# Third power of the far distance on GpSimd, parts of the near sum and of an edge mask on VectorE, in a convolution and spline kernel

## The chip, the cores and the metric

The kernel runs on one core of one Trainium2 chip. The metric is the device time of one execution in microseconds (us). Engines are named as in the profile: PE is TensorE, PEld its weight load, DVE is VectorE, ACT is ScalarE, POOL is GpSimd, SP is SyncE, which here only issues transfers.

## The reference

The input x has shape (32, 64, 56, 56). First comes a residual block with two 3x3 convolutions whose weights are replaced by their signs, each with a batch norm over the whole batch. Then each pixel goes through a cubic spline whose table of 32 knots is mixed per channel.

```python
out = relu(batchnorm(conv3x3(x, sign(w1)), gamma1, beta1))
x = relu(batchnorm(conv3x3(out, sign(w2)), gamma2, beta2) + x)
...
x_aff = clip(x * a + b, -1.5, 1.5)
u = (x_aff + 1) * 0.5 * (K - 1)              # K = 32
i = floor(u); t = clip(u - i, 0, 1)
spline = sum over k in 0..3 of alpha_table[clip(i - 1 + k, 0, 31)] * b_k(t)   # cubic B-spline basis
y_nl = einsum('bchwr,cr->bchw', spline, mix)
return id_gain * x + y_nl + bias
```

## The kernel before

Partitions hold 64 channels of two images. The function `convolutions` does both convolutions pair by pair, keeps the results in scratch tensors in HBM and builds the spline's coefficients beside them. The function `spline` then does the rest in 32 chunks (CHUNKS) of 1568 pixels (CHUNK, half an image), and almost all of the change is there.

Near a knot the spline is a cubic in the signed distance from that knot. For each pixel five coefficients are needed; the code calls them tables and numbers them T_NEAR, T_FAR, T_SQ, T_LIN and T_VAL: third power near the knot, third power of the distance beyond one cell (the far part), square, slope, value. A table is summed on PE: masks say which steps a pixel has passed, and matmuls of the masks with diagonal matrices of coefficient steps add the steps up in PSUM. There are four masks for each chunk. Two "middle" masks are made by VectorE (`middle`) and two "edge" masks by ScalarE (`edge`); each has four blocks of 1568 pixels. T_NEAR and T_FAR use all four masks and need 128 matmuls each, the others use the two edge masks and need 64 each, 448 together. Two PSUM tiles `tab` take turns, so PE may start a table when VectorE has consumed the one two before it (semaphore `table_used`).

VectorE consumes a table by adding the base and multiplying by a power of the distance, reading PSUM and one tile of SBUF: `near_cube`, `far_cube`, `square`, `slope`, `value`. `near_cube` leaves its product in `poly`; PE adds that product onto the T_SQ table in PSUM with 32 float32 matmuls with an identity matrix (`add_near_part`, eight for each quarter of the chunk), so that one multiplication by the squared distance in `square` serves both. `far_part` multiplies far distance times coefficient by the square of the far distance and by the constant AMP; a transfer with accumulation issued by GpSimd (`add_far`) adds it to the linear part `lin`. `add_slope` joins slope and square terms, and `finish` adds the polynomial to `lin`, which SP stores.

ScalarE computes positions, cell numbers, distance (`distance`, absolute value), far distance, its square, and the squared distance `dist_sq`, and scales the loaded data. The cell numbers are spread over blocks by 16 small transfers a chunk (`cell4<-cell`). On each engine the order of the steps is written out by hand; semaphores tie the engines together, and no scheduler has a say.

One VectorE step of the spline before:

```python
def far_part(c):
    dve.wait_ge(table_used, used(c, T_FAR))
    dve.wait_ge(lin_ready, c + 1)
    dve.scalar_tensor_tensor(out=far[c % 2][:, :], in0=far[c % 2][:, :], scalar=cc(AMP), in1=far_sq[:, :],
                             op0=ALU.mult, op1=ALU.mult).then_inc(far_part_ready, 1)
```

## Time and profile before

| what | us |
|---|---|
| median of three runs | 1126.56 |
| lowest and highest of them | 1124.85 and 1132.19 |
| time of the profiled execution | 1126.34 |
| its span in the profile | 1124.5 |
| PE busy | 1074.4 |
| VectorE busy | 963.5 |
| ScalarE busy | 899.2 |
| GpSimd busy | 170.2 |

The profiled execution is one run with the hardware profiler on; its own time lies 1.8 us above its span, since the span counts from the first to the last record. The busy times are averages over two stages that differ: up to about 411 us the convolutions, after that the spline. The chain of waits follows the work back from the last instruction.

### The profile page before, as it was taken

The numbers are of one execution on the slowest core, as the hardware profiler recorded it, in microseconds if no ns is written. First come the engines' busy times: TensorE is split into PE (matmuls) and PEld (weight loads), VectorE is DVE, ScalarE is ACT, GpSimd is POOL, SyncE is SP. The second block draws the span as 40 slices with busy tenths as digits, with TensorE's granted clock in tenths as the row PEclk, the third lists the DMA queues.
The fourth block names the chain that finished last, engine by engine and source line by source line (L and its number), as shares of the span: only waits on it lengthen the run. The fifth ranks groups of instructions, "written<-read, shape, count | busy, mean of one in ns | idle before, by whom it ended". The sixth has DMA issues, their size and how long they took to land.

```text
span 1124.5 us, 53088 instructions
## 1 busy us (share of the span) xinstructions
PE 1074.4 (96%) x24602; PEld 751.0 (67%) x24602; DVE 963.5 (86%) x931; ACT 899.2 (80%) x410; POOL 170.2 (15%) x236
## 2 busy tenths in 40 slices
PE   6999999799999968899999999999999999999996
PEld 5777777687777745566677666666666666666674
DVE  4865666686767779999999999999999999999986
ACT  4444544686777648999999999999999999999970
POOL 8388200000000000111011011110110111101100
PEclk9999999899999989999999999999999999999999
DMA  8577774777677946788888888889988888888642
GB/s 278 216 286 281 278 261 169 266 279 292 252 286 291 350 169 156 191 212 239 227 223 241 219 220 250 218 213 237 230 227 232 230 225 219 235 221 227 169 125 87
DMA packets 57335, 259.43 MB, mean 231 GB/s; under 512 B 15952, under 2 KB 15952, under 8 KB 49104
## 3 DMA queue, kind: packets, MB, share of 16 engines
q1 hardware_dynamic: 48368, 208.39, 52.1%
q0 software_dynamic: 8640, 48.17, 23.6%
q8 instruction: 147, 2.41, 0.9%
q10 hardware_dynamic: 160, 0.30, 0.1%
q14 instruction: 20, 0.16, 0.0%
HBM read 104.28 MB, written 77.07 MB: 161 GB/s over the span
## 4 chain that ended last, share of the span: by engine, by line
PE 94%; DVE 3%; issue 1%; DMA 1%; ACT 0%; ACTq 0%; DVEq 0%
PE tab L1334 52%; PE acc L771 34%; PE tab L1344 8%; DMA w_raw<-in_w 1%; DVE middle_mask L1192 0%; DVE far_sq L1241 0%; PE tab L1356 0%; DVE poly L1233 0%; DVE lin L1276 0%; DVE poly L1272 0%; DVE middle_mask L1201 0%; DVE stats L581 0%; ACT zbuf L1044 0%; DVE edge_mask L1201 0%; DVE offset L1185 0%
## 5 line engine op out<-in xcount | busy, mean ns | idle before, releaser
L1334 PE MATMUL tab<-edge_mask,diag 128*32 128x392 bf16 x10240 | 453.0, 329 | 9.7 <-issue 4.3
L1334 PEld LDWEIGHTS tab<-edge_mask,diag 128*32 128x32 f16 x10240 | 297.5, 97 | 153.5 <-issue 16.3
L1089 ACT ACTIVATE edge_mask<-cell,thr 128x6272 bf16<-128x6272 bf16 x62 | 338.8, 5513 | 2.1 <-DMA cell<-cell 2.1
L472 ACT ACTIVATE yout<-acc 128x1568 f32<-128x1568 f32 x64 | 94.5, 1477 | 162.9 <-PE acc L771 142.3
L771 PE MATMUL acc<-split,w 64*64 64x385 f16 (+3 forms) x4608 | 192.2, 327 | 11.5 <-DVE w L520 10.3
L771 PE MATMUL acc<-band_split,w 64*64 64x385 f16 (+3 forms) x4608 | 192.7, 327 | 6.5 <-DVE band_split L540 3.6
L599 DVE BATCH_NORM_STATS2 stats<-yout 128x392 f32 (+1 forms) x240 | 118.1, 556 | 93.1 <-ACT yout L472 93.1
L1334 PE MATMUL tab<-middle_mask,diag 128*32 128x392 bf16 x4096 | 187.2, 329 | 1.9 <-DVE middle_mask L1201 1.0
L771 PEld LDWEIGHTS acc<-split,w 64*64 64x64 f16 x4608 | 143.9, 108 | 59.0 <-issue 12.8
L771 PEld LDWEIGHTS acc<-band_split,w 64*64 64x64 f16 x4608 | 149.3, 108 | 49.6 <-issue 4.9
L1334 PEld LDWEIGHTS tab<-middle_mask,diag 128*32 128x32 f16 x4096 | 119.2, 97 | 56.7 <-issue 2.4
L1004 POOL DMA_DIRECT2D lin<-far x32 | 50.1, 1564 | 650.4 <-DVE far L1226 650.4
L1192 DVE TENSOR_SCALAR middle_mask<-cell,thr 128x6272 bf16<-128x6272 bf16 x62 | 114.6, 1848 | 0.0
L1344 PE MATMUL tab<-poly,ident 128*32 128x392 f32 x1024 | 92.7, 492 | 0.0
L999 POOL DMA_DIRECT2D lin<-in_x x28 | 32.3, 1153 | 257.7 <-ACT lin L1016 257.7
L1212 DVE SCALAR_TENSOR_TENSOR poly<-tab,first,poly 128x1568 f32<-128x1568 f32 x31 | 57.4, 1851 | 15.6 <-PE tab L1334 15.6
L1344 PEld LDWEIGHTS tab<-poly,ident 128*32 128x32 f32 x1024 | 46.1, 110 | 29.8 <-issue 16.5
L572 DVE SCALAR_TENSOR_TENSOR split<-split,xin 128x3136 f16<-128x3136 f16 (+4 forms) x19 | 55.0, 2907 | 10.1 <-ACT split L462 10.0
L1233 DVE SCALAR_TENSOR_TENSOR poly<-tab,first,dist_sq 128x1568 f32<-128x1568 f32 x31 | 57.3, 1848 | 3.8 <-PE tab L1344 3.6
L1226 DVE SCALAR_TENSOR_TENSOR far<-far,cst,far_sq 128x1568 f32<-128x1568 f32 x32 | 59.3, 1852 | 1.2
L1219 DVE SCALAR_TENSOR_TENSOR far<-tab,first,far 128x1568 f32<-128x1568 f32 x31 | 57.4, 1851 | 2.1 <-PE tab L1334 1.7
L1064 ACT ACTIVATE poly<-offset 128x1568 f32<-128x1568 int32 x32 | 48.4, 1513 | 12.7 <-DVE offset L1185 12.4
(151 smaller groups left out, 1013.7 us busy)
## 6 DMA issues: line engine op xcount, KB each, us to landing
y_scratch<-yout SPq DMA_DIRECT2D x32, 1568.0 KB, 6.1
cell<-cell SPq DMA_DIRECT2D x496, 98.0 KB, 4.0
xin<-y_scratch SPq DMA_DIRECT2D x16, 1568.0 KB, 6.2
lin<-far POOLq DMA_DIRECT2D x32, 784.0 KB, 8.6
out<-lin SPq DMA_DIRECT2D x31, 784.0 KB, 5.0
xin<-in_x SPq DMA_DIRECT2D x15, 1568.0 KB, 6.7
lin<-y_scratch SPq DMA_DIRECT2D x30, 784.0 KB, 8.4
lin<-in_x POOLq DMA_DIRECT2D x28, 784.0 KB, 8.3
```

Source lines behind the costliest of these rows:

```text
L472: act.activation(yout[b][:, :].rearrange("p (r k x) -> p k r x", r=2, k=TILES)[:, 2 * part:2 * part + 2], acc[:, 4 * part:4 * part + 4, 0: ...
L572: dve.scalar_tensor_tensor(out=inner(split[b][1], first, end), in0=inner(split[b][0], first, end), scalar=-SPLIT, in1=rows(xin[b], first, ...
L599: dve.bn_stats(stats[:, bass.ds(COUNTS * (g - base) + t, 1), :], yout[b][:, own]).then_inc(counted, 1)
L771: mm = pe.matmul(to[:, top:end, cols], weights[part][own, tap * C:(tap + 1) * C], image[own, first + dy + top:first + dy + end, from_cols] ...
L1089: act.activation(mask_of(c, q)[:, :, :], cell4[c % 2][:, :, :], ACT.Sign, bias=thr[:, q:q + 1]).then_inc(sign_mask_ready, 1)
L1192: dve.tensor_scalar(mask_of(c, q)[:, :, :], cell4[c % 2][:, :, :], thr[:, q:q + 1], None, ALU.is_ge).then_inc(mask_ready, 1)
L1212: dve.scalar_tensor_tensor(out=quarters(poly[c % 2]), in0=summed(c, T_NEAR), scalar=base(c, T_NEAR), in1=quarters(poly[c % 2]), op0=ALU.ad ...
L1219: dve.scalar_tensor_tensor(out=quarters(far[c % 2]), in0=summed(c, T_FAR), scalar=base(c, T_FAR), in1=quarters(far[c % 2]), op0=ALU.add, o ...
L1226: dve.scalar_tensor_tensor(out=far[c % 2][:, :], in0=far[c % 2][:, :], scalar=cc(AMP), in1=far_sq[:, :], op0=ALU.mult, op1=ALU.mult).then_ ...
L1233: dve.scalar_tensor_tensor(out=quarters(poly[c % 2]), in0=summed(c, T_SQ), scalar=base(c, T_SQ), in1=quarters(dist_sq), op0=ALU.add, op1=A ...
L1334: mm = pe.matmul(tab[(c + t) % 2][j * GROUP:(j + 1) * GROUP, sub, 0:SUB], keep["diag"][part][:, j % 2, t, q, :], mask_of(c, q)[:, j, sub * ...
L1344: mm = pe.matmul(tab[(c + T_SQ) % 2][j * GROUP:(j + 1) * GROUP, sub, 0:SUB], keep["ident"][:, j * GROUP:(j + 1) * GROUP], poly[c % 2][:, s ...
```

## The change

Five things are different, nearly all in `spline`.

The third power of the far distance no longer waits for the coefficient. ScalarE squares the far distance with a scale ROOT_AMP, GpSimd multiplies far distance and square (`far_third`), and `far_cube` of VectorE multiplies the coefficient onto that product. `far_part` is gone; for chunk 0 VectorE does the product itself (`first_far_third`). `far_third(c)` waits for `edge_block(c)` of VectorE and for `far_square(c)` of ScalarE, and stands in GpSimd's order behind the transfer of the far part of the chunk before.

PE adds the near part for three quarters of the chunk (PE_QUARTERS = 3), 24 matmuls in place of 32. For the last quarter VectorE adds the near part and the table in a second instruction in `square`, and multiplies by the squared distance in `rest_of_square`.

Block 3 of the first edge mask is made by VectorE (`edge_block`), ScalarE makes three blocks of it in place of four.

The orders on VectorE and ScalarE are written anew. `near_cube` uses the signed offset in place of the distance, ScalarE computes the distance straight into `far`, and the slope product goes into the offset's own tile (`sloped`) in place of `far_sq`.

In the setup AMP becomes a square of a power of two, with a few small instructions on VectorE, and GpSimd's `steps` gets one more small copy.

```diff
@@ convolutions, normalised_tables @@
+                bits = amax[:, :].bitcast(I32)
+                link(dve.tensor_scalar(bits, bits, 23, None, ALU.logical_shift_right), chain)
+                link(dve.tensor_scalar(bits, bits, 0.5, HALF_EXPONENT, ALU.mult, ALU.add), chain)
+                link(dve.tensor_scalar(bits, bits, 23, None, ALU.logical_shift_left), chain)
+                link(dve.tensor_copy(col(ROOT_AMP), amax[:, 0:1]), chain)
+                link(dve.tensor_tensor(amax[:, :], amax[:, :], amax[:, :], ALU.mult), chain)
                 link(dve.reciprocal(inv[:, :], amax[:, :]), chain)
-                link(dve.tensor_scalar(inv[:, :], inv[:, :], WIDEN, None, ALU.mult), chain)
                 link(dve.tensor_copy(col(INV_AMP), inv[:, 0:1]), chain)
-                link(dve.tensor_scalar(col(AMP), amax[:, 0:1], 1 / WIDEN, None, ALU.mult), chain)
+                link(dve.tensor_copy(col(AMP), amax[:, 0:1]), chain)
...
@@ spline, sync @@
                 wait_past(sp, sign_mask_ready, edge_masks(c - 2))
+                wait_past(sp, edge_block_ready, c - 2)
@@ spline, gpsimd @@
+            def far_third(c):
+                pool.wait_ge(edge_block_ready, c)
+                pool.wait_ge(far_sq_ready, c + 1)
+                pool.tensor_tensor(far[c % 2][:, :], far[c % 2][:, :], far_sq[:, :],
+                                   ALU.mult).then_inc(far_third_ready, 1)
             def add_far(c):
-                pool.wait_ge(far_part_ready, c + 1)
+                pool.wait_ge(table_used, used(c, T_FAR))
+                pool.wait_ge(lin_ready, c + 1)
                 pool.dma_start(lin_of(c)[:, :], far[c % 2][:, :], accum_op=ALU.add).then_inc(far_added, 16)
             for c in range(CHUNKS):
                 if AHEAD <= c + 3 < CHUNKS:
                     add_x(c + 3)
                 add_far(c)
+                if c + 1 < CHUNKS:
+                    far_third(c + 1)
@@ spline, scalar @@
             def edge(c, q):
-                act.activation(mask_of(c, q)[:, :, :], cell4[c % 2][:, :, :], ACT.Sign,
+                blocks = slice(0, 3 if q == EDGE_QUADS[0] else 4)
+                act.activation(mask_of(c, q)[:, blocks, :], cell4[c % 2][:, blocks, :], ACT.Sign,
@@ spline, vector @@
+            def edge_block(c):
+                dve.wait_ge(copied[c % 2], copies(c))
+                wait_past(dve, table_ready, TABLES * (c - 1))
+                q = EDGE_QUADS[0]
+                dve.tensor_scalar(mask_of(c, q)[:, 3, :], cell4[c % 2][:, 3, :], keep["above"][:, q:q + 1], 2.0,
+                                  ALU.is_ge, ALU.mult).then_inc(edge_block_ready, 1)
...
             def square(c):
+                most, rest = slice(0, PE_QUARTERS), slice(PE_QUARTERS, 4)
                 dve.wait_ge(dist_sq_ready, c + 1)
+                dve.wait_ge(table_used, used(c, T_NEAR))
                 dve.wait_ge(table_ready, used(c, T_SQ))
-                dve.scalar_tensor_tensor(out=quarters(poly[c % 2]), in0=summed(c, T_SQ), scalar=base(c, T_SQ),
-                                         in1=quarters(dist_sq), op0=ALU.add,
-                                         op1=ALU.mult).then_inc(table_used, 1)
+                dve.scalar_tensor_tensor(out=quarters(poly[c % 2])[:, most, :], in0=summed(c, T_SQ)[:, most, :],
+                                         scalar=base(c, T_SQ), in1=quarters(dist_sq)[:, most, :], op0=ALU.add,
+                                         op1=ALU.mult).then_inc(square_parts, 1)
+                dve.scalar_tensor_tensor(out=quarters(poly[c % 2])[:, rest, :], in0=quarters(poly[c % 2])[:, rest, :],
+                                         scalar=1 / POINT, in1=summed(c, T_SQ)[:, rest, :], op0=ALU.mult,
+                                         op1=ALU.add).then_inc(table_used, 1)
+            def rest_of_square(c):
+                own = slice(PE_QUARTERS * SUB, CHUNK)
+                dve.wait_ge(table_used, used(c, T_SQ))
+                dve.scalar_tensor_tensor(out=poly[c % 2][:, own], in0=poly[c % 2][:, own], scalar=base(c, T_SQ),
+                                         in1=dist_sq[:, own], op0=ALU.add, op1=ALU.mult).then_inc(square_ready, 1)
@@ spline, tensor @@
                 if t == T_SQ:
                     pe.wait_ge(table_used, used(c, T_NEAR))
-                    for sub in range(4):
+                    for sub in range(PE_QUARTERS):
                         mm = add_near_part(c, sub)
```

Now the order of the instructions, first on VectorE in a steady chunk. The names are tiles: `poly` the polynomial, `far` the far part, `offset` the signed distance, `zbuf` the position, `lin` the linear part. A step with `tab` among its inputs consumes a table. Before:

```order
L1177 TENSOR_SCALAR zbuf<-zbuf,cst 128x1568
L1171 TENSOR_SCALAR lin<-lin,cst,par_sb 128x1568
L1212 SCALAR_TENSOR_TENSOR poly<-tab,first,poly 128x1568
L1261 SCALAR_TENSOR_TENSOR lin<-poly,cst,lin 128x1568
L1192 TENSOR_SCALAR middle_mask<-cell,thr 128x6272
L1219 SCALAR_TENSOR_TENSOR far<-tab,first,far 128x1568
L1226 SCALAR_TENSOR_TENSOR far<-far,cst,far_sq 128x1568
L1192 TENSOR_SCALAR middle_mask<-cell,thr 128x6272
L1233 SCALAR_TENSOR_TENSOR poly<-tab,first,dist_sq 128x1568
L1185 TENSOR_SCALAR offset<-zbuf 128x1568
L1241 SCALAR_TENSOR_TENSOR far_sq<-tab,first,offset 128x1568
L1247 SCALAR_TENSOR_TENSOR poly<-far_sq,poly 128x1568
```

After, from the near step on:

```order
L1250 SCALAR_TENSOR_TENSOR poly<-tab,first,offset 128x1568
L1214 TENSOR_SCALAR offset<-zbuf 128x1568
L1200 TENSOR_SCALAR lin<-lin,cst,par_sb 128x1568
L1221 TENSOR_SCALAR middle_mask<-cell,thr 128x6272
L1262 SCALAR_TENSOR_TENSOR far<-tab,first,far 128x1568
L1221 TENSOR_SCALAR middle_mask<-cell,thr 128x6272
L1229 TENSOR_SCALAR edge_mask<-cell,above 128x1568
L1271 SCALAR_TENSOR_TENSOR poly<-tab,first,dist_sq 128x1176
L1274 SCALAR_TENSOR_TENSOR poly<-poly,tab 128x392
L1291 SCALAR_TENSOR_TENSOR offset<-tab,first,offset 128x1568
L1282 SCALAR_TENSOR_TENSOR poly<-poly,first,dist_sq 128x392
L1299 SCALAR_TENSOR_TENSOR poly<-offset,poly 128x1568
```

The multiplication of the far part (`far<-far,cst,far_sq`) has gone, the block of the edge mask and three pieces of the square have come, offsets and linear part stand ahead of the first middle mask, and `finish` (`lin<-poly,cst,lin`) stands ahead of the near step except in chunk 1. The first middle mask stood ahead of the far step before as well.

The second place is ScalarE in a steady chunk. Before:

```order
L1089 ACTIVATE edge_mask<-cell,thr 128x6272 x2
L1064 ACTIVATE poly<-offset 128x1568
L1027 ACTIVATE zbuf<-lin,cst 128x1568
L1070 ACTIVATE far<-poly,cst 128x1568
L1016 ACTIVATE lin<-lin,cst 128x1568
L1076 ACTIVATE far_sq<-far 128x1568
L1083 ACTIVATE dist_sq<-offset 128x1568
L1038 ACTIVATE cell<-zbuf,cst 128x1568
```

After:

```order
L1115 ACTIVATE edge_mask<-cell,thr 128x4704
L1091 ACTIVATE far<-offset 128x1568
L1096 ACTIVATE far<-far,cst 128x1568
L1102 ACTIVATE far_sq<-far,cst 128x1568
L1115 ACTIVATE edge_mask<-cell,thr 128x6272
L1054 ACTIVATE zbuf<-lin,cst 128x1568
L1043 ACTIVATE lin<-lin,cst 128x1568
L1108 ACTIVATE dist_sq<-offset 128x1568
L1065 ACTIVATE cell<-zbuf,cst 128x1568
```

Distance, far distance and its square now stand between the two edge masks, one behind the other, and a whole edge mask and four steps stand between the square of the far distance and the next chunk's masks.

## Rows read from the trace of the kernel before

**Rows 1.** the page, part 1: busy us, share of the span, instructions

```profile
PE 1074.4 (96%) x24602; PEld 751.0 (67%) x24602; DVE 963.5 (86%) x931; ACT 899.2 (80%) x410; POOL 170.2 (15%) x236
```

**Rows 2.** chain that ended last, steady chunks: start us, us, what

```profile
486.65 2.63 PE tab L1344 x32
489.28 18.57 PE tab L1334 x448
...
1107.70 2.63 PE tab L1344 x32
```

**Rows 3.** windows over one chunk: length, then busy us of each engine

```profile
602.41:623.62 21.21, 21.21 (x488) 15.49 (x480) 20.83 (x14) 21.21 (x10) 2.77 (x2) 1.00 0.89 231
```

**Rows 4.** timeline of VectorE, one steady chunk: start us, us, engine, line

```profile
606.55 1.85 DVE L1212 SCALAR_TENSOR_TENSOR poly<-tab,first,poly 128x1568 f32<-128x1568 f32 x1 [0.27 <-PE tab L1334]
...
611.85 1.85 DVE L1219 SCALAR_TENSOR_TENSOR far<-tab,first,far 128x1568 f32<-128x1568 f32 x1
613.74 1.85 DVE L1226 SCALAR_TENSOR_TENSOR far<-far,cst,far_sq 128x1568 f32<-128x1568 f32 x1
615.51 1.85 DVE L1192 TENSOR_SCALAR middle_mask<-cell,thr 128x6272 bf16<-128x6272 bf16 x1
...
619.91 1.85 DVE L1241 SCALAR_TENSOR_TENSOR far_sq<-tab,first,offset 128x1568 f32<-128x1568 f32 x1
621.79 1.79 DVE L1247 SCALAR_TENSOR_TENSOR poly<-far_sq,poly 128x1568 f32<-128x1568 f32 x1
```

**Rows 5.** groups of VectorE, 418 to 450: count, busy us, mean ns

```profile
L1201 DVE TENSOR_SCALAR edge_mask<-cell,above 128x3136 bf16<-128x3136 bf16 x4 | 4.0, 1030 | 0.0
...
L1192 DVE TENSOR_SCALAR middle_mask<-cell,thr 128x6272 bf16<-128x6272 bf16 x2 | 3.7, 1848 | 0.0
```

**Rows 6.** timeline of VectorE, closing quarters

```profile
1117.47 0.63 DVE L1276 SCALAR_TENSOR_TENSOR lin<-poly,cst,lin 128x392 f32<-128x392 f32 x1
1118.01 0.62 DVE L1272 SCALAR_TENSOR_TENSOR poly<-tab,first,poly 128x392 f32<-128x392 f32 x1
```

**Rows 7.** timeline of ScalarE, one steady chunk

```profile
609.12 10.93 ACT L1089 ACTIVATE edge_mask<-cell,thr 128x6272 bf16<-128x6272 bf16 x2
620.03 1.51 ACT L1064 ACTIVATE poly<-offset 128x1568 f32<-128x1568 int32 x1
621.45 1.68 ACT L1027 ACTIVATE zbuf<-lin,cst 128x1568 f32<-128x1568 f32 x1
```

**Rows 8.** timeline of ScalarE, chunk 0, a step behind its own input

```profile
425.99 1.51 ACT L1064 ACTIVATE poly<-offset 128x1568 f32<-128x1568 int32 x1 [1.17 <-DVE offset L1185]
427.54 1.61 ACT L1070 ACTIVATE far<-poly,cst 128x1568 f32<-128x1568 f32 x1
```

**Rows 9.** timeline of GpSimd, steady chunk: issue of the far part

```profile
615.89 1.59 POOL L1004 DMA_DIRECT2D lin<-far  x1 [9.49 <-DVE far L1226]
```

**Rows 10.** timeline of GpSimd, first convolution

```profile
24.75 1.41 POOL L389 TENSOR_TENSOR w_signs<-w_signs,w_below 128x576 f32<-128x576 f32 x1
...
58.28 0.21 POOL L344 TENSOR_TENSOR dsel<-dsel,own_step 128x10 f32<-128x10 f32 x1
...
78.29 0.36 POOL L401 TENSOR_SCALAR diag<-ident,dlo 128x32 f16<-128x32 f32 x1
78.75 3.55 POOL L401 TENSOR_SCALAR diag<-ident,dhi 128x32 f16<-128x32 f32 x1
```

**Rows 11.** timeline of VectorE, same stretch of the first convolution

```profile
78.64 3.42 DVE L572 SCALAR_TENSOR_TENSOR split<-split,xin 128x3136 f16<-128x3136 f16 x1 [0.62 <-ACT split L462]
```

**Rows 12.** timeline of VectorE, chunk 1

```profile
457.01 1.85 DVE L1212 SCALAR_TENSOR_TENSOR poly<-tab,first,poly 128x1568 f32<-128x1568 f32 x1
...
467.71 1.85 DVE L1233 SCALAR_TENSOR_TENSOR poly<-tab,first,dist_sq 128x1568 f32<-128x1568 f32 x1
```

**Rows 13.** timeline of TensorE, chunk 1

```profile
469.61 2.84 PE L1334 MATMUL tab<-edge_mask,diag 128*32 128x392 bf16 x64 [2.57 <-DVE poly L1233]
```

**Rows 14.** transfers issued by the far part's line (L1004), landing

```profile
DMA to landing us min/median/max: 5.8/8.6/9.9
```

104 lines of the change are left out of this document (64 added, 40 removed).

## The prediction

> **What bounds the kernel now.** I read the page first. PE is busy for 1074.4 us of 1124.5, but VectorE with 963.5 and ScalarE with 899.2 are not far behind [rows 1], and these are means over two stages. So the chain of waits comes next, in the spline. It alternates between 448 bf16 matmuls in 18.57 us and 32 float32 matmuls of the near part in 2.63 us, 21.20 us a chunk, and from chunk 2 to chunk 31 hardly anything else is on it [rows 2]: 1107.70 - 486.65 = 621.05 us are 29 rounds of 21.20 (614.8) and 6.2 us of small gaps. The third view is a window exactly one round long: PE 21.21 of 21.21, ScalarE 21.21, VectorE 20.83 [rows 3]. The reader is to see that three engines are full at once. Taking work from PE gains only what the other two can follow, so each engine's round after the change has to be added up.
>
> **PE.** The near part shrinks from 32 to 24 matmuls: 2.63 x 3/4 = 1.97 us. PE's round becomes 18.57 + 1.97 = 20.54, which is 0.66 less.
>
> **VectorE.** Its round has one wait of 0.27 us, in front of the near step [rows 4], so 20.93 is work. Steps are counted start to start. `far_part` goes: 615.51 - 613.74 = 1.77, and the far step in front of it shrinks from 1.89 to 1.77, since nothing then waits for its result at once [rows 4]: 1.89 less. The edge block is new. The same instruction takes 1030 ns for 3136 elements and 1848 for 6272 [rows 5], so a block of 1568 lasts 1030 - 409 = 0.62, of which the next step overlaps 0.08 (615.59 against 615.51): 0.54 more. A step on a quarter costs 1118.01 - 1117.47 = 0.54 [rows 6]; `square` in two pieces costs 0.13 more than 1.77, and `rest_of_square` 0.54. The 0.12 that `add_slope` waits for its input (1.88 from the slope's start to its own) [rows 4] it now waits for `rest_of_square`. Sum: 20.93 - 1.89 + 0.54 + 0.13 + 0.54 = 20.25, under PE's 20.54 by 0.29, nearly the slack of today.
>
> The deadlines inside a round hold as well. PE may start T_VAL when `square` is through; that leaves VectorE 2.65 us (a quarter of the 448 matmuls' time for 64) behind the near part, and the two pieces take 1.90. The middle masks, the near step and the far step all come later than their tables or masks allow. Putting offsets and linear part ahead of the first middle mask moves steps inside the round and costs nothing while the middle masks of the next chunk are due half a round later. The middle mask stood ahead of the far step already: that part of the change does nothing.
>
> **ScalarE.** It is full: two edge masks in 10.91 (609.12 to 620.03), distance in 1.42 [rows 7], the rest of the 21.20 in six steps. One block less of an edge mask saves 1568 elements; from 10.93 / 2 = 5.46 for 6272 and 1.51 for 1568, a block is (5.46 - 1.51) / 3 = 1.32. Distance, far distance and square now follow each other, and a step behind its own input starts 1.55 after it [rows 8] in place of 1.42: 0.13 twice, and up to 0.1 for the scale read from a tile. Sum: 21.20 - 1.32 + 0.36 = 20.24. That too fits in 20.54, and the wait for the fixed positions takes up the rest.
>
> **GpSimd and the pair that it shares with VectorE.** The multiplication of 128x1568 float32 is new. In the trace 128x576 took 1.41 and 128x10 took 0.21 [rows 10], 2.12 ns an element: 0.21 + 3.30 = 3.51 us. Its wait is tied to the edge block. GpSimd began 0.30 after the end of the VectorE step that it waited for (613.74 + 1.85 = 615.59, then 615.89) [rows 4, 9]. Counted from the start of the edge block it thus begins at 0.62 + 0.30 = 0.92 and ends at 4.43. VectorE runs `square` and `slope`, which read PSUM and one SBUF tile, until 0.54 + 1.90 + 1.77 = 4.21, and then `rest_of_square` with two SBUF inputs. Does this matter? A small GpSimd step of 0.36 took 3.55 when a VectorE step with two SBUF inputs ran over it, and ended 0.24 behind that one's end (82.30 against 82.06) [rows 10, 11]. So GpSimd is held by VectorE. No row shows VectorE held by GpSimd; I assume that it works both ways, and then `rest_of_square` is held for 4.43 - 4.21 = 0.22 and a hand-over. Bounds: nothing, if only GpSimd gives way or starts 0.1 after the block; 0.45 with the whole 0.24. I take 0.3, in the middle. A further 0.05 I set for GpSimd's issues of transfers, which now meet the edge block (the far part's issue lasted 1.59 under a middle mask [rows 4, 9]) and `finish`. VectorE's round is then 20.25 + 0.35 = 20.6, just above PE's 20.54. The gain of a round is 0.6.
>
> The Trainium skill, page "SBUF — State Buffer", section "SBUF: two separate sides", speaks against the change: the shared pair is an exclusive lock, and whichever of the two engines starts first keeps it for the whole instruction while the other fully blocks. The trace agrees for one direction, GpSimd held for 3.55 us [rows 10, 11]; by the rule the hold on VectorE is certain, without it the round would be PE's 20.54. The page "GPSIMD Engine Reference", section "Elementwise — side-by-side cycle accounting", gives 4497 ns for an add of 2048 float32; an estimate from it is 3.44 us for 1568, which would shorten the hold by 0.07.
>
> **Start of the spline.** In chunk 1 PE waited 2.57 us for the square step of chunk 1, which ran 467.71 to 469.56 [rows 12, 13]. VectorE is what counts here. Up to the end of that step it loses two far parts (1.77 + 1.89) and gains the first far third (1.77, and 0.12 since the far step waits for it), two edge blocks (1.08), two split squares (0.26), `rest_of_square` of chunk 0 (0.66 with the wait for its result) and the offsets of chunk 2 (0.88, now ahead): 4.77 - 3.66 = 1.1 later. In addition, far distance and square of chunk 1 are ready some 2 us ahead of the near step at 457.01 [rows 12], among short VectorE steps, and behind the near step stands `finish` with two SBUF inputs. If GpSimd starts with the near step, `finish` is held for 3.51 - 1.77 = 1.74; if it slips in earlier, up to 3.5; if VectorE keeps its turn, nothing. I take 1.8.
>
> **End, setup, transfers.** Behind the last slope the chain has `rest_of_square` more: 0.54. The setup adds some small VectorE instructions and one of GpSimd, under a us, in a stage where VectorE idles in front of each split step [rows 11] and PE sets the pace: nothing. If that cover were gone, it would be under 1 us. Bytes and transfers are the same. The far part's transfer lands at most 9.9 us after its issue [rows 14]; it is issued 0.3 behind the far step, 1.4 ahead of the edge block's start, and lands by 8.5 on that clock, while `finish` comes at 9.8 (4.5 for what is summed above, then 0.66, 1.8, 1.8 and 1.0). It is a smaller margin than now, and each us beyond it would cost one. SP's spread also waits for an edge block, one that is two chunks old. The loading of x stands behind the multiplication on GpSimd, but a chunk ahead of its use.
>
> **Sum.** 30 rounds x 0.6 = 18.0, less 1.1, 1.8 and 0.5 = 14.6 us. The profiled execution had 1126.34, its span and 1.8 us around it, and agrees with the median of 1126.56 within 0.2, so: 1126.5 - 14.6 = 1112.
>
> **The rivals.** PE stays the bound: VectorE is never held, or is served first. For it speaks that the multiplication fits into `square` and `slope` but for 0.22; against it, that nothing is left over. 30 x 0.66 - 1.1 - 0.5 = 18.2: 1108. Chance 0.25.
>
> The meetings on the pair eat the gain. GpSimd has three instructions a chunk, and masks, positions, `finish`, `add_slope` may each be held for some tenths. With 0.7 to 0.9 us held in a round it is 20.95 to 21.15: a gain of 1.5 to 7.5, less 3.4, is 1122 to 1128, take 1125. Against it: with the issues of today no VectorE step is seen held. Chance 0.18.
>
> Slower than before: the square of the far distance comes too late. Place: `far_third` behind `far_square` on ScalarE. From the fixed positions ScalarE needs four steps of 1.5 to 1.6 and three blocks of an edge mask (5.46 - 1.32 = 4.14), 10.3 us, to the square; VectorE needs five steps of 1.77, the offsets (0.9), a linear part (1.1) and the edge block, 11.4, so the square is 1.1 ahead; ScalarE has 0.3 of slack in a round, and if it falls behind VectorE's clock the margin is used up. From there each us that GpSimd starts late holds `rest_of_square` and `add_slope` for one us more. It decides from 20.25 + 0.85: beyond that the kernel is slower. At 1.5 us held the round is 21.75: +16.5 and 3.4 are 1146. Chance 0.15.
>
> The forecast has 0.42, and covers 1109 to 1117.
>
> **How the numbers follow.** The range runs from the PE bound with an easy start, 1106, to the end of the third case, 1128, and leaves out the slow case. One per cent, what a measurement of this kernel can tell from no change, is 11.3 us: faster is below 1115.3. PE bound 0.25 and nine tenths of the forecast give 0.63; the third case and the rest of the forecast give 0.21; the slow case with the edge of the third 0.16.
>
> **What would show it.** In the changed kernel's chain: 24 float32 matmuls in 1.97 us. In the timeline of VectorE: rounds of 20.5 to 20.7; `rest_of_square` starting 0.1 to 0.5 after the slope step should end, in the same instant in which GpSimd's multiplication ends; 3.5 us for that multiplication. In ScalarE's waits: some tenths before the cells, none of PE for the edge masks. In chunk 1: `finish` held for 1.8 us. I would be wrong if the multiplication took 4 us or more, if VectorE were held at places not named here, or if `far_third` waited for ScalarE.

## The result, and the profile after

The changed kernel took 1121.03 us (median of 20 runs, 1115.86 to 1134.65), the kernel before 1126.85 (20 runs beside them). The ratio is 0.9948, with an interval from 0.9931 to 0.9964: 5.9 us faster where 14.6 were forecast. One execution of the 20, 1134.65, was a slow one and is left out of the ratio, as such executions are in every ratio below. The profiled execution of the changed kernel had 1119.22 and a span of 1117.1, so the spans lie 7.4 us apart; what follows accounts for those 7.4.

The page of the changed kernel, one row each of parts 1, 3 and 5; PE's row answers to [rows 1]:

```profile
PE 1055.1 (94%) x24346; PEld 726.6 (65%) x24346; DVE 947.0 (85%) x999; ACT 868.6 (78%) x410; POOL 287.9 (26%) x268
...
q8 instruction: 146, 2.39, 0.9%
...
L1022 POOL TENSOR_TENSOR far<-far,far_sq 128x1568 f32<-128x1568 f32 x31 | 110.9, 3578 | 22.3 <-ACT far_sq L1102 12.2
```

PE is busy for 19.3 us less than before, near the 32 x 0.66 = 21 of the removed matmuls. The span shrank by only 7.4, so some 12 us have turned into idle time of PE. The granted clock of TensorE is 1.00 from 700 to 900 us in both kernels, so the clock has no part in it. GpSimd's multiplication took 3.58 us on average. The chain of waits says where PE's time went; its columns are start, length, work. It answers to [rows 2]:

```profile
533.43 18.57 PE tab L1395 x448
552.00 1.98 PE tab L1405 x24
...
637.50 6.68 PE tab L1395 x160
644.18 2.09 issue
646.28 12.12 PE tab L1395 x288
658.40 1.98 PE tab L1405 x24
...
1100.28 1.98 PE tab L1405 x24
```

An undisturbed round is 18.57 + 1.98 = 20.55 us, as forecast for PE. The round from 637.50 to 660.37 is not: after 160 matmuls PE stands for 2.09 us, the chain names nothing that it waited for ("issue"), and the round is 22.87 long. TensorE's waits from 486 to 1100, by releaser, which is what ended the wait (us in total, times, longest), first of the changed kernel and then of the kernel before:

```profile
PE tab L1395 <- issue: 9.6, 11, 2.1
```

```profile
PE tab L1334 <- issue: 3.5, 6, 1.2
```

No wait for VectorE or ScalarE is left in either. What has grown is the wait with no releaser, from 3.5 to 9.6 us. From the near part of chunk 2 to that of chunk 31 the chain has 489.87 to 1100.28 = 610.41 us; 29 undisturbed rounds are 595.8, so 14.6 us are lost, against 6.2 before (the prediction's first paragraph has that count). I call what the 29 rounds take beyond undisturbed ones the excess below. Part of it is idle time named "issue"; the rest sits inside matmul pieces that run longer than their count allows.

The two rounds of VectorE's timeline around 600 us answer to [rows 4] (start, length, line, operation, in brackets the idle time before it and its releaser):

```profile
595.25 0.62 DVE L1229 TENSOR_SCALAR edge_mask<-cell,above 128x1568 bf16<-128x1568 bf16 x1
...
599.10 1.85 DVE L1291 SCALAR_TENSOR_TENSOR offset<-tab,first,offset 128x1568 f32<-128x1568 f32 x1 [0.74 <-PE tab L1395]
600.87 0.62 DVE L1282 SCALAR_TENSOR_TENSOR poly<-poly,first,dist_sq 128x392 f32<-128x392 f32 x1
601.63 1.79 DVE L1299 SCALAR_TENSOR_TENSOR poly<-offset,poly 128x1568 f32<-128x1568 f32 x1
...
616.92 0.62 DVE L1229 TENSOR_SCALAR edge_mask<-cell,above 128x1568 bf16<-128x1568 bf16 x1
617.46 1.44 DVE L1271 SCALAR_TENSOR_TENSOR poly<-tab,first,dist_sq 128x1176 f32<-128x1176 f32 x1
618.81 0.56 DVE L1274 SCALAR_TENSOR_TENSOR poly<-poly,tab 128x392 f32<-128x392 f32 x1
619.64 1.85 DVE L1291 SCALAR_TENSOR_TENSOR offset<-tab,first,offset 128x1568 f32<-128x1568 f32 x1 [0.28 <-PE tab L1395]
621.41 0.62 DVE L1282 SCALAR_TENSOR_TENSOR poly<-poly,first,dist_sq 128x392 f32<-128x392 f32 x1
```

And GpSimd's timeline beside it, which answers to [rows 9]:

```profile
593.87 1.58 POOL L1029 DMA_DIRECT2D lin<-far  x1 [9.15 <-DVE far L1262]
595.96 3.56 POOL L1022 TENSOR_TENSOR far<-far,far_sq 128x1568 f32<-128x1568 f32 x1 [0.50 <-DVE edge_mask L1229]
603.86 0.88 POOL L1016 DMA_DIRECT2D lin<-in_x  x1 [4.34 <-ACT lin L1043]
615.55 2.12 POOL L1029 DMA_DIRECT2D lin<-far  x1 [10.81 <-DVE far L1262]
617.68 3.58 POOL L1022 TENSOR_TENSOR far<-far,far_sq 128x1568 f32<-128x1568 f32 x1
```

The multiplication starts at 595.96, which is 0.09 after the edge block ends (595.25 + 0.62 = 595.87), and is over at 599.52. `rest_of_square` starts at 600.87 with its usual 0.62: it is not held. In the next round the multiplication starts later, since the issue of the far part in front of it lasted 2.12, and ends at 621.26, still ahead of `rest_of_square` at 621.41. Instead of being the bound VectorE waits for PE in front of the slope step, 0.74 and 0.28.

At the start of the spline VectorE's timeline (to set beside [rows 12]) has:

```profile
456.34 4.32 DVE L1206 TENSOR_SCALAR zbuf<-zbuf,cst 128x1568 int32<-128x1568 f32 x1
460.58 1.84 DVE L1250 SCALAR_TENSOR_TENSOR poly<-tab,first,offset 128x1568 f32<-128x1568 f32 x1
...
467.76 1.83 DVE L1262 SCALAR_TENSOR_TENSOR far<-tab,first,far 128x1568 f32<-128x1568 f32 x1
```

GpSimd's in the same stretch:

```profile
455.63 4.20 POOL L1022 TENSOR_TENSOR far<-far,far_sq 128x1568 f32<-128x1568 f32 x1 [12.21 <-ACT far_sq L1102]
```

TensorE's, beside [rows 13]:

```profile
462.48 2.84 PE L1395 MATMUL tab<-edge_mask,diag 128*32 128x392 bf16 x64 [2.51 <-DVE poly L1250]
...
469.65 2.84 PE L1395 MATMUL tab<-edge_mask,diag 128*32 128x392 bf16 x64 [2.36 <-DVE far L1262]
473.77 2.50 PE L1395 MATMUL tab<-edge_mask,diag 128*32 128x392 bf16 x56 [1.28 <-DVE poly L1274]
```

The step at 456.34 is `fixed`, the fixed positions of the chunk ahead. It takes 1.09 us elsewhere and 4.32 here, and it ends 0.83 behind the multiplication (455.63 + 4.20 = 459.83). PE then waits three times for VectorE, 6.15 us in all, and its value table of chunk 1 starts at 473.77 in place of 469.61: 4.2 later.

So the 7.4 us are: +4.2 at the start; -0.9 between there and the near part of chunk 2, where the kernel before had a gap of 0.75 that the changed one has not; -10.6 in 29 rounds; and nothing at the end, where the shorter last near part (-0.65) pays for `rest_of_square` behind the last slope. From the end of the last matmul (1104.93, and 1113.00 before) to the end of the span it is 12.2 against 11.5: +0.7.

### The profile page after: what moved, and what is told of

Same layout as the page of the kernel before. It is cut to its first block, busy times and chain, and to the rows that moved or that the text cites. A ratio compares the mean times of both kernels' runs of the same rounds, so it can differ in the third digit from the quotient of the medians.

```text
span 1117.1 us, 52831 instructions
## 1 busy us (share of the span) xinstructions
PE 1055.1 (94%) x24346; PEld 726.6 (65%) x24346; DVE 947.0 (85%) x999; ACT 868.6 (78%) x410; POOL 287.9 (26%) x268
## 4 chain that ended last, share of the span: by engine, by line
PE 91%; DVE 5%; issue 2%; DMA 1%; ACT 0%; ACTq 0%; DVEq 0%
PE tab L1395 51%; PE acc L780 34%; PE tab L1405 5%; DMA w_raw<-in_w 1%; DVE middle_mask L1221 1%; DVE edge_mask L1238 0%; DVE poly L1250 0%; DVE offset L1291 0%; DVE poly L1299 0%; DVE middle_mask L1238 0%; PE tab L1417 0%; DVE offset L1214 0%; DVE lin L1328 0%; DVE poly L1324 0%; DVE stats L584 0%
## 5 line engine op out<-in xcount | busy, mean ns | idle before, releaser
L1395 PE MATMUL tab<-edge_mask,diag 128*32 128x392 bf16 x10240 | 450.9, 329 | 13.8 <-issue 4.4
L1395 PEld LDWEIGHTS tab<-edge_mask,diag 128*32 128x32 f16 x10240 | 289.2, 97 | 165.8 <-issue 18.1
L1115 ACT ACTIVATE edge_mask<-cell,thr 128x4704 bf16<-128x4704 bf16 (+1 forms) x62 | 300.9, 4855 | 4.0 <-DMA cell<-cell 4.0
L1029 POOL DMA_DIRECT2D lin<-far x32 | 55.0, 1720 | 646.4 <-DVE far L1262 323.2
L780 PE MATMUL acc<-band_split,w 64*64 64x385 f16 (+2 forms) x4608 | 192.1, 327 | 6.5 <-DVE band_split L543 3.6
L780 PEld LDWEIGHTS acc<-split,w 64*64 64x64 f16 x4608 | 145.6, 108 | 58.1 <-issue 13.6
L1022 POOL TENSOR_TENSOR far<-far,far_sq 128x1568 f32<-128x1568 f32 x31 | 110.9, 3578 | 22.3 <-ACT far_sq L1102 12.2
L1405 PE MATMUL tab<-poly,ident 128*32 128x392 f32 x768 | 70.7, 492 | 0.0
L1291 DVE SCALAR_TENSOR_TENSOR offset<-tab,first,offset 128x1568 f32<-128x1568 f32 x31 | 57.4, 1850 | 14.9 <-PE tab L1395 14.9
L1065 ACT ACTIVATE cell<-zbuf,cst 128x1568 bf16<-128x1568 uint16 x31 | 49.7, 1602 | 25.8 <-DVE zbuf L1206 25.8
L1299 DVE SCALAR_TENSOR_TENSOR poly<-offset,poly 128x1568 f32<-128x1568 f32 x32 | 57.4, 1793 | 4.5
L1250 DVE SCALAR_TENSOR_TENSOR poly<-tab,first,offset 128x1568 f32<-128x1568 f32 x31 | 57.1, 1843 | 2.7 <-PE tab L1395 2.7
```

Of the source, the lines that this page charges most:

```text
L780: mm = pe.matmul(to[:, top:end, cols], weights[part][own, tap * C:(tap + 1) * C], image[own, first + dy + top:first + dy + end, from_cols] ...
L1022: pool.tensor_tensor(far[c % 2][:, :], far[c % 2][:, :], far_sq[:, :], ALU.mult).then_inc(far_third_ready, 1)
L1115: act.activation(mask_of(c, q)[:, blocks, :], cell4[c % 2][:, blocks, :], ACT.Sign, bias=thr[:, q:q + 1]).then_inc(sign_mask_ready, 1)
L1250: dve.scalar_tensor_tensor(out=quarters(poly[c % 2]), in0=summed(c, T_NEAR), scalar=base(c, T_NEAR), in1=quarters(offset[c % 2]), op0=ALU. ...
L1291: dve.scalar_tensor_tensor(out=quarters(sloped(c)), in0=summed(c, T_LIN), scalar=base(c, T_LIN), in1=quarters(offset[c % 2]), op0=ALU.add, ...
L1299: dve.scalar_tensor_tensor(out=poly[c % 2][:, :], in0=sloped(c), scalar=1 / POINT, in1=poly[c % 2][:, :], op0=ALU.mult, op1=ALU.add).then_ ...
```

## The experiments

Each is an edit of the changed kernel ("after") or of the kernel before. Ratios are to the kernel before, timed on the same chip in turn. This table holds what was measured: TensorE's idle time without releaser from 486 to 1100 us, the time from the near part of chunk 2 to that of chunk 31 in TensorE's timeline, and the excess of that over 29 undisturbed rounds (614.8 where PE does four quarters, 595.8 where it does three).

| kernel | median us (runs) | ratio, interval | PE idle, "issue" | 29 rounds | excess |
|---|---|---|---|---|---|
| before | 1126.85 (20) | 1 | 3.5 | 620.9 | 6.1 |
| after | 1121.03 (20) | 0.9948 [0.9931, 0.9964] | 9.6 | 610.4 | 14.6 |
| e0_after_again | 1120.39 (12) | 0.9945 [0.9922, 0.9968] | 9.1 | 610.2 | 14.4 |
| e1_after_light | 1120.70 (9) | 0.9925 [0.9899, 0.9951] | 7.6 | 608.9 | 13.1 |
| e2_before_light | 1126.30 (12) | 0.9985 [0.9969, 1.0002] | 2.4 | 620.0 | 5.2 |
| e3_third_dve_c1 | 1120.33 (6) | 0.9938 [0.9916, 0.9959] | 10.6 | 611.3 | 15.5 |
| e4_pe4 | 1139.95 (4) | 1.0117 [1.0081, 1.0154] | 7.7 | 627.6 | 12.8 |
| e5_pe2 | 1111.12 (4) | 0.9864 [0.9838, 0.9890] | 4.2 | 601.2 | |
| e8_small_third | 1115.13 (4) | 0.9898 [0.9872, 0.9924] | 5.6 | 606.8 | 11.0 |
| e9_small_addx | 1112.15 (4) | 0.9871 [0.9846, 0.9896] | 2.2 | 601.7 | 5.9 |
| e13_before_small_addx | 1125.97 (10) | 0.9989 [0.9972, 1.0005] | 3.4 | 620.3 | 5.5 |
| e10_addx_after_cells | 1125.94 (12) | 0.9985 [0.9967, 1.0003] | 13.6 | 617.7 | 21.9 |
| e14_before_scale_early | 1132.03 (12) | 1.0057 [1.0037, 1.0077] | 7.6 | 626.8 | 12.0 |
| e15_after_scale_late | 1118.50 (6) | 0.9931 [0.9911, 0.9952] | 8.2 | 608.3 | 12.5 |
| e16_pe2_scale_late | 1112.13 (6) | 0.9882 [0.9860, 0.9904] | 9.8 | 606.4 | |
| e11_pe2_third | 1113.53 (6) | 0.9891 [0.9863, 0.9918] | 6.6 | 604.2 | |
| e6_third_dve | 1148.38 (4) | 1.0184 [1.0153, 1.0216] | 12.8 | 640.7 | |
| e7_no_edge_block | 1129.45 (10) | 1.0021 [1.0004, 1.0037] | 0.9 | 621.9 | |

### Where PE's gaps are

Before any edit I counted matmuls along the chain. Every instruction pair (a weight load and a matmul) counts one. In the changed kernel the gaps stand at these positions modulo 128: 3, 2, 0, 126, 126, 124, 122, 118, 116, 113, 111, 110; in the kernel before at 38, 37, 35, 33, 30, 30, 28, 26. I take the slow drift for the few other instructions of PE, which the count leaves out. So a gap can only come once in 256 instructions of PE. The page has a queue of kind "instruction" with 146 packets of 16.4 KB on average (q8). From 411 us on the trace has 119 of them for 15,120 matmuls and as many weight loads, which are some 118 times 256 instructions; in the kernel before it has 120 for 120 times 256. (In the convolutions it has 27 for 72 times 256; why they are fewer there stays open.) I read a gap as a batch of PE's instructions that lands too late.

The packets' own times in the traces bear this out. The gap from 644.18 to 646.28 ends 1.24 us after the end of a packet of q8 at 645.04. In the 18 traces of this document PE has 180 such gaps between 486 and 1100 us, and each of them ends 1.0 to 1.6 us after the end of a q8 packet, while these packets are 5.7 us apart on average. At the boundaries without a gap the last packet has mostly landed long before, 3.0 us in the changed kernel (median). The Trainium skill, page "Runtime: NRT & Kernel Launch", section "Instruction fetch mechanics", says of these batches that an engine's instructions are refilled in blocks of 256, by transfers of the engine's own, at a cost that is "mostly hidden". The positions and the packet count of the spline agree with the 256; the cost here is up to 2.09 us a block.

The traces also show which packets are late. Each of the 180 started either 5.9 to 9.5 us after GpSimd issued the transfer of a far part, or 4.4 to 10.1 us after it issued that of x. 940 packets fall into these stretches; of the 1003 that fall outside, none was late. The stretches were drawn around the gaps afterwards, so they describe and predict nothing; but where the transfer of x is cut (e9 and e13 below) all gaps left, 4 and 6, are behind a far part. Both transfers take some 8.5 us from issue to landing (median), so the late packets are those that start around such a landing.

That leaves why the batches land later after the change, whose bytes are the same. Four reasons were in question: the load on the DMA queues as such; the held start and GpSimd's multiplication, with the gaps a side matter; PE's faster pace, which asks for batches earlier; and the reordered steps, which start their transfers at other places of the round. The expectations quoted below name them as they stood when each was written: theory A is the load of all transfers, B anything else, C GpSimd's long multiplication, D the place of the transfer of x in the round, E PE's faster pace beside a full VectorE.

### The load, and a repeat: e0, e1, e2

```diff
-sp.dma_start(image_half(out, c), lin_of(c)[:, :])
+sp.dma_start(image_half(out, c)[:, 0:98], lin_of(c)[:, 0:98])
```

e1 makes this edit in the changed kernel and e2 in the kernel before: all but 98 of 1568 columns of the chunks' output are left unwritten. e0 is the changed kernel again.

> The changed kernel again on the same chip, as the measure for the others of this call: 1118 to 1124, gaps of PE between 486 and 1100 of 6 to 13 us, at the same phase of 128 matmuls as in the first profile.

> The changed kernel; each chunk's result store but the last sends 98 of 1568 columns, so most of the output is not written. Theory A: PE's unnamed gaps, 9.6 us between 486 and 1100 in the changed kernel, are refills of its instructions that come late because the transfers fill the DMA engines. With 23 MB less to move they fall under 3 us, the rounds are 20.55 to 20.65, and the time falls from 1121 to 1110 to 1114. Theory B: the gaps come from elsewhere (GpSimd's multiplication, the tighter hand-over between VectorE and PE) and stay at 8 to 10 us, the time above 1118.

> The kernel before with the same cut of the stores. Theory A: its gaps of 3.5 us fall under 1.5 and the time from 1126.8 to 1121 to 1124, so that the two light kernels lie 10 to 13 us apart, twice the 5.9 of the full ones. Theory B: the distance between the light kernels stays at 5 to 7 us.

The repeat has the same gaps in kind and sum (9.1 against 9.6), so they belong to the kernel. With a tenth of the bytes less they shrink a little in both kernels (9.6 to 7.6, 3.5 to 2.4), and the two stay as far apart as they were: excess 13.1 against 5.2. Load alone does not explain the difference.

### The held start: e3

```diff
 # GpSimd
-if c + 1 < CHUNKS:
+if 1 < c + 1 < CHUNKS:
     far_third(c + 1)
 # VectorE, chunk 1
 if c == 1:
     near_cube(c)
+    first_far_third(c)
```

> The changed kernel, but VectorE multiplies the far part of chunk 1 as well, behind its near step. Theory: the 4.32 us of the fixed step of chunk 3, in place of 1.09, is VectorE held by GpSimd's multiplication. Then it is 1.09 again, VectorE has one step of 1.8 more, and PE's value table of chunk 1 starts 1.4 us earlier; time 1 to 2 us under the changed kernel. Rival: the step was slow for another reason; it stays at 4.3 and the kernel is 1.8 slower.

VectorE's timeline of e3:

```profile
456.38 1.09 DVE L1206 TENSOR_SCALAR zbuf<-zbuf,cst 128x1568 int32<-128x1568 f32 x1
...
466.27 1.84 DVE L1262 SCALAR_TENSOR_TENSOR far<-tab,first,far 128x1568 f32<-128x1568 f32 x1
```

`fixed` is back at 1.09, so the multiplication had held it. Its own multiplication costs VectorE 1.7, and `far_cube` of chunk 1 starts at 466.27 in place of 467.76. The gain of 1.5 does not last: PE loses it there again (7.15 us for 128 matmuls from 468.17 on, where 5.48 are usual, and a gap of 0.98 at 485.05), the near part of chunk 2 starts at 489.69 as in the changed kernel at 489.70, and no gain shows in the time. That what is won in one place meets the next late batch is a guess from this one run.

### The size of GpSimd's multiplication: e8

```diff
-pool.tensor_tensor(far[c % 2][:, :], far[c % 2][:, :], far_sq[:, :], ALU.mult)
+pool.tensor_tensor(far[c % 2][:, 0:98], far[c % 2][:, 0:98], far_sq[:, 0:98], ALU.mult)
```

The other 1470 columns keep the distance without its square; VectorE's own steps are the same.

> The changed kernel, but GpSimd multiplies only 98 of 1568 columns, so the far part is wrong in the rest. The DMA load explains only a part of PE's gaps (9.1 and 9.6 us in the changed kernel, 7.6 with light stores; 3.5 and 2.4 before). Theory C: the long multiplication itself brings the gaps; they fall to 3 to 4 us and the time to 1112 to 1115 (3.2 us of that from chunk 1, where VectorE is no longer held). Theories D and E: the gaps stay at 8 to 10 and only the 3.2 us of chunk 1 are won, 1117.

It is 5.9 us faster than the changed kernel. `fixed` of chunk 1 is at 1.09 again and `far_cube` starts at 464.98, 2.8 earlier; the remaining 3.6 lie in the rounds, whose excess falls from 14.6 to 11.0, while no VectorE step of a steady round was held to begin with. Nor did the multiplication delay GpSimd's transfers: those of x and of the far part start 8.60 and 19.24 us behind the end of the near part in e8 (medians), and 8.62 and 19.25 in the changed kernel.

### The transfer of x: e9 and e13

```diff
-pool.dma_start(lin_of(c)[:, :], image_half(x, c), accum_op=ALU.add)
+pool.dma_start(lin_of(c)[:, 0:98], image_half(x, c)[:, 0:98], accum_op=ALU.add)
```

In both, x is added in 98 of 1568 columns only (in chunks 4 to 31, where GpSimd issues it); e9 is the changed kernel, e13 the kernel before.

> The changed kernel, but the accumulating transfer of x brings 98 of 1568 columns, so from chunk 4 on the spline gets the wrong input. Most gaps of the changed kernel begin 7 to 8 us into the round of PE that starts with the slope table, just when this transfer starts. Theory D: the place of that transfer against the refills makes the gaps; they fall under 4 us, time 1113 to 1116. Theories C and E: 7 to 9 us remain, as with the light stores.

> The kernel before, with the transfer of x cut to 98 of 1568 columns (wrong input from chunk 4 on). Its gaps fall from 3.5 to under 2 us and the time to 1122 to 1125. The changed kernel with the same cut took 1112.15: then the distance of the two is 10 to 13 us, what 30 rounds of 0.66 less 4.2 at the start and 0.6 at the end give (15), less some, against 6 for the full kernels. If the gaps of before were as costly in x, it would be under 1120.

TensorE's waits, of e9 and then of e13:

```profile
PE tab L1395 <- issue: 2.2, 4, 1.0
```

```profile
PE tab L1334 <- issue: 3.4, 6, 1.0
```

The changed kernel falls by 8.9 us to 1112.15, and the kernel before by next to nothing. With x cut the two lie 1125.97 - 1112.15 = 13.8 us apart (13.3 with some 3.4 either way by the ratios), and the excess is 5.9 against 5.5. That is the forecast of 14.6 within what was measured, but the match of the total proves no term of it: the profiled executions of the two lie 16.0 apart, and their 29 rounds 18.5 where 17.4 were forecast. The DMA share of the window from 700 to 900 us fell from 0.88 to 0.75 in e9 and from 0.87 to 0.73 in e13, so the load is as equal as before; only the changed kernel gains from the cut.

### The place of that transfer: e10, e14, e15

e10 holds the transfer back in the changed kernel, so that it starts 12.2 us behind the end of a near part instead of 8.6 (median over the chunks; 9.4 in the kernel before):

```diff
 pool.wait_ge(scaled, c - AHEAD + 1)
+pool.wait_ge(cell_ready, c)
 pool.dma_start(lin_of(c)[:, :], image_half(x, c), accum_op=ALU.add)
```

e14 moves one ScalarE step of the kernel before ahead, which moves the transfer from 9.4 to 7.9:

```diff
-far_distance(c)
 if AHEAD <= c + 3 < CHUNKS:
     scale(c + 3)
+far_distance(c)
 far_square(c)
```

e15 moves `scale` behind `distance_square` in the changed kernel: 10.0 in place of 8.6.

> The changed kernel, but GpSimd issues the transfer of x only when ScalarE has made the cell numbers, about 4 us later in the round; everything is moved and computed as before. If the place of that transfer against PE's refills makes the gaps, they change clearly from 9 to 10.6 us: under 5 us (time 1114 to 1117), as the transfer is then further from the far part's. If it is the load of the DMA engines as a whole, they stay at 8 to 11 and the time at 1119 to 1122.

> The kernel before, with ScalarE's scale step one place earlier (1.5 us), and with it GpSimd's transfer of x: it begins 7.9 us into PE's round in place of 9.4, nearer to the far part's. If the place of this transfer makes the gaps, they rise from 3.5 (2.4 and 3.4 in its relatives) to 6 us or more, and the time by 3 us or more, to 1130. If it is something else in the changed kernel, gaps of 2.4 to 4 and a ratio within 0.998 to 1.002.

> The changed kernel with the scale step behind the squared distance, 1.4 us later; the transfer of x begins 10.0 us into the round in place of 8.6, close to the 9.4 of before. If the place makes the gaps: 3 to 6 us of gaps, time 1114 to 1118. If not: 9 to 11 us, 1119 to 1122. With 4 us later (12.2) they were 13.6.

TensorE's waits in e14:

```profile
PE tab L1334 <- issue: 7.4, 10, 1.4
PE tab L1344 <- issue: 0.2, 1, 0.2
```

e14 is the sharpest run. One ScalarE step of the kernel before stands one place earlier and `far_distance` one later; no byte, no matmul and no VectorE step differs, the far part's transfer stays at 20.07 us (median), PE's undisturbed round is 21.20 still, and the kernel is 5.8 us slower, with 7.6 us of gaps and an excess of 12.0. e10 is 4.9 us slower than the changed kernel. So the place matters, by as much as the change lost. But it isn't a matter of early or late: e15, whose transfer is nearest to where it was before, is at 8.2 us of gaps, and its time isn't shown to differ from the changed kernel's. My expectation for it missed.

### The pace, and how the near part is shared: e4 and e5

```diff
-PE_QUARTERS = 3
+PE_QUARTERS = 4   # e4, without rest_of_square and its waits; 2 in e5
```

> The changed kernel with the near part of all four quarters on PE again (32 float32 matmuls, no second square piece, no rest of square). PE's round is 21.20; VectorE has 19.1 and ScalarE 20.2 of it. Theory E: the gaps come with the faster pace of PE and with full VectorE; here they are 3 to 4 us, and the time is 1127 to 1131 (before, plus 2 to 4 us of chunk 1). Theories C and D: the gaps are 8 to 10 us at a round of 21.2, and the time 1133 to 1137.

> The changed kernel with two quarters of the near part on VectorE: PE's round is 19.9, VectorE's 20.27 + 0.82 = 21.1, so VectorE sets the pace and PE has 1.2 us to spare in each round. If the gaps of PE cost time only while PE is the bound, the rounds are an even 21.1 and the 30 of them 633 us, against 631 in the changed kernel: time 1121 to 1125. If VectorE's round is longer than summed, above 1128.

e4 is the changed kernel with all four quarters of the near part on PE. Its round is that of the kernel before, 21.20, and it is slower than that kernel by 13, more than either theory had given it: its near part of chunk 2 starts 6.0 later and its excess is 12.8. So the faster pace is not needed for them: gaps grew at the old pace too. And the quarter that VectorE took over is worth 1139.95 - 1121.03 = 18.9. That this is so near 29 rounds of 0.66 (19.1) is partly luck: 17.2 lie in the 29 rounds, whose excess is 1.8 smaller in e4, and 2.8 at the start, where e4's 6.0 against 3.2 isn't explained.

e5 gives VectorE a second quarter. VectorE's timeline:

```profile
609.46 0.96 DVE L1214 TENSOR_SCALAR offset<-zbuf 128x1568 int32<-128x1568 int32 x1
...
618.12 0.95 DVE L1274 SCALAR_TENSOR_TENSOR poly<-poly,tab 128x784 f32<-128x784 f32 x1
...
620.76 1.02 DVE L1282 SCALAR_TENSOR_TENSOR poly<-poly,first,dist_sq 128x784 f32<-128x784 f32 x1
...
630.06 0.96 DVE L1214 TENSOR_SCALAR offset<-zbuf 128x1568 int32<-128x1568 int32 x1
```

And TensorE's waits:

```profile
PE tab L1395 <- DVE poly L1274: 12.4, 19, 1.0
PE tab L1395 <- issue: 4.2, 9, 1.3
```

VectorE's round is now 630.06 - 609.46 = 20.60 and sets the pace; PE's own would be 18.57 + 1.32 = 19.89. I had expected 21.1, since I counted 0.5 and more for the second quarter; it costs 0.41 (1.02 against 0.62 in `rest_of_square`; 1.02 + 0.95 against 1.44 + 0.55 in `square`, which is nothing). PE has 0.71 us of slack in a round, shown as 12.4 us of waits for VectorE, which late batches use up first. 4.2 us of gaps are left, and 29 rounds take 601.2, which is 20.73 each and 3.8 more than 29 x 20.60. At 1111.12 it is the fastest version, 9.9 us below the changed kernel and 15.8 below the kernel before.

### Two attempts to better it: e11, e16

e11 adds e3's edit to e5, e16 adds e15's.

> Two quarters of the near part on VectorE, and the third power of chunk 1 by VectorE as well. VectorE sets the pace with rounds of 20.7, PE has 0.8 us to spare for its refills. Expected: as with two quarters alone (1111.1) less 0 to 1.5 us for chunk 1: 1110. If the start is hidden anyway, 1111.

> Two quarters of the near part on VectorE and the scale step late. As VectorE sets the pace and PE has 0.8 us to spare, gaps count little: 1109 to 1112, the same as with two quarters alone (1111.1) or 1 us less.

Neither is better than e5 (0.9891 and 0.9882 against 0.9864); over 29 x 20.60 they have 6.8 and 9.0. So with the slack the loss is smaller than the changed kernel's 14.6, but it still depends on where the transfers fall. What the slack does is seen by setting the loss beside the named gaps: it is 2.1 to 8.3 us more than they are in the thirteen rows above where PE alone sets the pace (5.0 in the changed one), and within 0.8 of them in e5, e11 and e16 (3.8 beside 4.2, 6.8 beside 6.6, 9.0 beside 9.8). At equal gaps it saves some 5 us, as e16 shows; the rest of e5's gain is that it has fewer gaps, which the slack doesn't explain. Leaving the multiplication of chunk 1 to VectorE shows no gain in either kernel (e3, e11).

### What the other parts are worth: e6, e7

e6 leaves the multiplication to VectorE in every chunk: GpSimd's `far_third` goes, and VectorE calls `first_far_third(c)` ahead of the first middle mask. In e7 ScalarE makes all four blocks of the edge mask and VectorE copies one column in place of the block; the fourth block then holds 1 and -1 where the base constants count on 2 and 0, so its sums are shifted.

```diff
-blocks = slice(0, 3 if q == EDGE_QUADS[0] else 4)
+blocks = slice(0, 4)
```

> The changed kernel with the third power of every chunk by VectorE, none by GpSimd. VectorE's round is 20.27 + 1.77 = 22.05, 0.85 above the round of before: 30 x 0.85 = 25 us over it, less 0 for the start: 1150 to 1154. PE's unnamed gaps cost nothing there, as PE waits for VectorE. If GpSimd's multiplication had a hidden price in every round, the kernel would be nearer, under 1145.

> The changed kernel with the whole edge mask by ScalarE; VectorE has a copy of one column in place of the edge block, to keep the signal. ScalarE's round is 20.3 + 1.3 = 21.6 and sets the pace: 30 x 0.4 = 12 us over the round of before, with the start 1135 to 1141. If ScalarE were not that full, 1120.

Without GpSimd's multiplication VectorE sets the pace (29 rounds in 640.7, 22.09 each, undisturbed ones 21.87) and the kernel is slower than before, 1148.38: against the changed kernel's 1121.03 the multiplication on GpSimd buys 27 us. Without the edge block ScalarE sets the pace (29 rounds in 621.9, 21.44 each; it is busy for 21.43 us of a round of 21.50) and the change gains nothing: 1.0021. I had expected 1135 or more, since I put its round too high. PE's gaps are 0.9 us there, yet 12.8 in e6, where PE waits for VectorE too (21.7 us): waiting for another engine does not by itself make the gaps go. They cost less there: 29 x 21.87 is 634.2, so the excess is 6.5 beside 12.8 us of gaps. Each of the three engines was relieved by what it needed, as the prediction counted.

e7 shows one thing more, the hold that the prediction assumed. ScalarE's square of the far distance comes late there, so GpSimd's multiplication starts late. One round of VectorE, and GpSimd's beside it:

```profile
709.31 1.84 DVE L1290 SCALAR_TENSOR_TENSOR offset<-tab,first,offset 128x1568 f32<-128x1568 f32 x1
711.07 2.43 DVE L1281 SCALAR_TENSOR_TENSOR poly<-poly,first,dist_sq 128x392 f32<-128x392 f32 x1
```

```profile
709.52 3.55 POOL L1022 TENSOR_TENSOR far<-far,far_sq 128x1568 f32<-128x1568 f32 x1 [1.88 <-ACT far_sq L1102]
```

`rest_of_square`, a step with two SBUF inputs that takes 0.62 alone, takes 2.43 and ends 0.43 behind the multiplication (709.52 + 3.55 = 713.07); this happens in 29 rounds, where it takes 1.44 to 2.43 us (2.40 in the median) and ends 0.42 to 0.43 behind the multiplication each time. The slope step in front, which reads PSUM and one SBUF tile, keeps its 1.84.

## Why the prediction was right and wrong

**Right: PE's round.** 18.57 + 1.97 forecast, 20.54 to 20.55 in the chain; e4, without it, takes 17.2 us more for the 29 rounds.

**Right: the work of VectorE and ScalarE.** From 599.10 to 619.64 VectorE has 20.54 with 0.28 of waiting, so 20.26 of work where 20.25 was forecast. ScalarE's waits:

```profile
ACT cell L1065 <- DVE zbuf L1206: 23.2, 27, 2.5
```

That is 0.86 a round. 20.24 of work was forecast for it; 0.30 under PE's 20.54, with the 14.6 us of excess shared out over 29 rounds (0.50), makes 0.80.

**Off by a size: the hold in a round.** I set 0.3 for `rest_of_square` held by GpSimd and 0.05 beside it, which made VectorE the bound at 20.6. The hold is nil: from chunk 2 on every `rest_of_square` takes 0.61 to 0.62 us and starts 1.76 to 1.77 after the slope step. The assumption behind it, that GpSimd can hold VectorE too, is right (e7). GpSimd started 0.09 after the edge block, not the 0.30 read from an issue of a transfer [rows 9], and VectorE's wait for PE in front of the slope step put `rest_of_square` behind the multiplication's end. The rival that PE stays the bound was the better description of a round; it would have added 29 x 0.06 = 1.7 us to the gain.

**Off by a size: the start.** 1.1 + 1.8 = 2.9 forecast, 4.2 measured. VectorE as the loser is confirmed: 4.32 in place of 1.09 at 456.34, and 1.09 in e3 and e8. By the rule of the Trainium skill, page "SBUF — State Buffer", section "SBUF: two separate sides", which the prediction weighed, the later of the two fully blocks, where VectorE's step has two SBUF inputs or runs in what the page calls a 2-port perf mode; the trace agrees, now in the direction that no row of the kernel before showed. But it was `fixed`, a step with one SBUF input, and not `finish`. No run shows its mode; it does 1568 float32 in 1.09 us where steps with two inputs take 1.85. Most of the multiplication lay over it: 3.2 instead of 1.8. The bound "up to 3.5" held it.

**Right: the end.** 0.54 forecast, 0.7 measured. The far square is in time: from chunk 2 on the multiplication waits for the edge block or for nothing, so the slower case had no part in it; e7 shows its mechanism, where the square is late.

**The term that failed: the gaps of PE, carried over as if nothing could move them.** The prediction read "6.2 us of small gaps" in the chain of before, said "Bytes and transfers are the same", and its sum has no term for them. The excess went from 6.2 to 14.6, 8.4 us, and nearly the whole miss is that: of a forecast 17.4 us in 29 rounds 10.6 came. It would have been 19.1 with the gaps of before. That the time of 1121.03 lies inside the stated range is luck: its upper part was there for steps held on the shared pair, and no steady round had one. That the term moves with transfers, and needs neither PE's new pace nor a held VectorE, is shown: with the x transfer cut in both kernels they lie 13.8 us apart (e9, e13); at the old pace the gaps are there as well (e4); a single ScalarE step moved in the kernel before costs 5.8 us of the same kind (e14).

**Open.** That a gap is a batch of instructions landing late rests on its positions modulo 128 and on the end of a q8 packet 1.0 to 1.6 us before the end of each of the 180 gaps; no run changed the batches themselves. The late ones start around the landings of GpSimd's two transfers. But why more of them are late after the change isn't found: in both kernels 57 packets of some 108 fall into the stretches named above, and 11 were late against 6. e10, e14 and e15 move x's transfer by -1.5 to +3.6 us, and the gaps don't grow or shrink with it in one direction. The multiplication on GpSimd adds to them too (e8), by a way that I can't name.

## What to carry to other kernels

When an engine is alone on the chain and runs its instructions at full pace, read the waits that have no releaser as a term of the sum, and ask what moves them; any edit that shifts the place of transfers in the round can change it by several us though it changes no byte. Try a version in which such an engine isn't the only bound: with 0.7 us of slack in each round the late batches were cheaper here by some 5 us, and handing VectorE one more quarter gained 10 us in all, though the count of work alone (20.60 against 20.54 a round) promised nothing. Place a GpSimd step with SBUF inputs over VectorE steps that read PSUM: over `fixed` it cost VectorE 3.2 us once, and over `rest_of_square` 1.8 us a round in e7.
